# The parts of a group's row maxima in one 128-column tile: one transpose and four small DMAs in place of four transposes and one DMA

## The reference

```
scores  = einsum('bhqd,bhkd->bhqk', q, k) / sqrt(16)      # 4 x 16 x 512 x 512
weights = softmax(scores, axis=-1)
attn    = einsum('bhqk,bhkd->bhqd', weights, v)
```

## Time and profile before

| | us |
|---|---|
| median of 3 runs | 1273.53 (1271.52 to 1274.54) |
| the profiled execution: its own time | 1274.43 |
| its span, first to last instruction | 1272.7 |
| attend stage of xa0, sa0, xa1 (about) | 72 to 340, 414 to 630, 945 to 1155 |
| PE busy | 1131.4 (89% of the span) |
| DVE, ACT, POOL busy | 838.6 (66%), 660.4 (52%), 210.9 (17%) |
| mean granted clock of PE | 0.949 |

### The profile page before, as it was taken

How to read it: one execution, slowest core, us unless ns; L and a number is a source line. 1 busy time by engine, 2 the same in 40 slices (tenths; PEclk the granted TensorE clock), 3 DMA queues, 4 the chain that set the end, 5 groups by cost and what they waited for, 6 DMA issues and landing times. The chain is left out here.

```text
span 1272.7 us, 17810 instructions
## 1 busy us (share of the span) xinstructions
PE 1131.4 (89%) x5693; PEld 544.0 (43%) x5722; DVE 838.6 (66%) x2112; ACT 660.4 (52%) x1341; POOL 210.9 (17%) x272
## 2 busy tenths in 40 slices
PE   7889999999997999999967999996989999998390
PEld 4423343434453223343364666664523333335370
DVE  5878777777478888888762222223888888876722
ACT  3346666666533677677722333332537767674250
POOL 4310000000143000000202222211520010102154
PEclk9989999999999899999967999998989999999795
DMA  8953321221048433543291140103873323211064
GB/s 265 309 169 93 79 57 28 81 52 26 2 154 291 103 91 90 132 97 93 72 375 33 31 161 28 27 13 102 263 241 91 90 59 89 60 37 57 25 171 144
DMA packets 100706, 139.40 MB, mean 110 GB/s; under 512 B 8452, under 2 KB 82632, under 8 KB 99208
## 3 DMA queue, kind: packets, MB, share of 16 engines
q1 hardware_dynamic: 96536, 128.03, 33.6%
q0 software_dynamic: 4080, 10.23, 2.9%
HBM read 86.30 MB, written 52.17 MB: 109 GB/s over the span
## 5 line engine op out<-in xcount | busy, mean ns | idle before, releaser
L885 ACT ACTIVATE r<-ps 128x512 f32<-128x512 f32 x768 | 427.4, 600 | 211.9 <-PE ps L971 122.1
L377 DVE TENSOR_REDUCE m<-ps 128x1 f32<-128x512 f32 x512 | 320.9, 682 | 45.2 <-PE ps L958 44.9
L971 PE MATMUL ps<-r 99*128 99x512 bf16 x768 | 294.3, 388 | 5.6 <-ACT r L885 5.6
L958 PE MATMUL ps<-r 96*128 96x512 bf16 x720 | 280.9, 393 | 20.5 <-DVE m L377 7.0
L373 DVE CUSTOM_DVE_ANT_0 r<-ps,r 128x512 bf16<-128x512 f32 x256 | 170.2, 690 | 60.2 <-PE ps L958 59.6
L985 PE MATMUL ps<-r 128*32 128x512 f32 x1536 | 204.9, 605 | 4.9 <-ACT r L885 3.3
L971 PEld LDWEIGHTS ps<-r 99*128 99x128 bf16 x768 | 74.4, 98 | 211.7 <-ACT r L885 157.3
L958 PEld LDWEIGHTS ps<-r 96*128 96x128 bf16 x720 | 71.3, 99 | 105.9 <-DVE m L377 24.3
L861 POOL COPY r<-r 128x256 f32<-128x256 f32 x48 | 19.0, 399 | 542.1 <-PE ps L985 542.1
L1660 DVE COPY r<-ps 128x512 f32<-128x512 f32 x46 | 31.8, 691 | 91.9 <-PE ps L1707 91.9
L1707 PE MATMUL ps<-r 128*128 x184 | 87.8, 621 | 2.7 <-issue 0.4
(11 more groups left out here) (151 smaller groups left out, 1220.5 us busy)
## 6 DMA issues: line engine op xcount, KB each, us to landing
r<-q_parts SPq DMA_DIRECT2D x48, 384.0 KB, 5.2
r<-k_parts SPq DMA_DIRECT2D x48, 384.0 KB, 6.0
k_parts<-r SPq DMA_DIRECT2D x24, 384.0 KB, 3.3
q_parts<-r SPq DMA_DIRECT2D x24, 384.0 KB, 3.1
r<-in_w SPq DMA_DIRECT2D x16, 512.0 KB, 4.9
r<-in_w SPq DMA_DIRECT2D x8, 1024.0 KB, 14.4
k_parts<-r SPq DMA_DIRECT2D x24, 256.0 KB, 3.3
q_parts<-r SPq DMA_DIRECT2D x24, 256.0 KB, 3.1
```

What stands on the lines that cost most here:

```text
L377: ins = dve.tensor_reduce(out, mem.ps[:, bank, :], AX.X, ALU.max)
L885: act.activation(mem.probs[:, u // HG, u % HG, :], ps[:, ST + (UNITS * g + u) % DEEP, :], ACT.Exp, scale=SCALE).then_inc(a.p_exp.sem, 1)
L958: pe.matmul(ps[:, led_bank(n), :], mem.qst[g][0:ROWS, h, t * P:(t + 1) * P], mem.kst[g][0:ROWS, h, :], start=True, stop=True).then_inc(a.s ...
L971: ins = pe.matmul(out, mem.kst[g][0:KROWS, h, kt * P:(kt + 1) * P], mem.qst[g][0:KROWS, h, :], start=True, stop=not a.masked)
```

## The change

`mparts` becomes a tile of 128 columns, of which 48 carry the parts (4 tiles x 3 parts x 4 heads) and the rest is zero from the start. PE turns it with one transpose: 48 partitions x 128. ACT copies 48 x 128 elements in place of 12 x 512. SP sends the four tiles' parts with four DMAs, each of 12 partitions x 128 (3 KB, in runs of 256 bytes), and the semaphore of the shift counts to 64 in place of 16. POOL has one memset more at the start, and those who wait for the constants wait for 14.

```diff
-        self.mparts = sb("mparts", [P, T, PARTS, HG], BF16)
-        self.mT = sb("mT", [PARTS * HG, S], BF16)
+        self.mparts = sb("mparts", [P, P], BF16)
+        self.mT = sb("mT", [PARTS * T * HG, P], BF16)
...
-        self.shift = [sig(f"shift{s}", 16) for s in range(NG)]
+        self.shift = [sig(f"shift{s}", 16 * T) for s in range(NG)]
...
         sp.wait_ge(a.m_sb.sem, a.m_sb.at(G, 1))
-        sp.dma_start(mem.qst[g][ROWS:KROWS, :, :], mem.mT[:, :]).then_inc(a.shift[g].sem, 16)
+        for t in range(T):
+            sp.dma_start(mem.qst[g][ROWS:KROWS, :, t * P:(t + 1) * P],
+                         mem.mT[t * PARTS * HG:(t + 1) * PARTS * HG, :]).then_inc(a.shift[g].sem, 16)
...
-        act.activation(mem.mT[:, :], ps[0:PARTS * HG, MISC, 0:S // 2].bitcast(BF16), ACT.Copy)\
+        act.activation(mem.mT[:, :], ps[0:PARTS * T * HG, MISC, 0:P // 2].bitcast(BF16), ACT.Copy)\
            .then_inc(a.m_sb.sem, 1)
...
-        for t in range(T):
-            ins = pe.transpose(ps[0:PARTS * HG, MISC, t * P // 2:(t + 1) * P // 2].bitcast(BF16),
-                               mem.mparts[:, t, :, :].rearrange("p a h -> p (a h)"), mem.identb[:, :])
-        ins.then_inc(a.m_ps.sem, 1)
+        pe.transpose(ps[:, MISC, 0:P // 2].bitcast(BF16), mem.mparts[:, :], mem.identb[:, :]).then_inc(a.m_ps.sem, 1)
...
+        mparts = mem.mparts[:, 0:T * PARTS * HG].rearrange("p (t a h) -> p t a h", t=T, a=PARTS)
+        hi, mid, lo = (mparts[:, :, i, :] for i in range(PARTS))
...
+            pool.memset(mem.mparts[:, :], 0.0).then_inc(setup, 1)
```

More of the change, by code:

```diff
@@ L715, in rest_of_batches @@
         if a.fresh:
-            sp.wait_ge(a.setup, 13)
+            sp.wait_ge(a.setup, 14)
             for s in range(NG):
@@ L896, in maxima @@
             b, g = used
-            act.wait_ge(a.shift[g].sem, a.shift[g].at(b, 16))
-        act.activation(mem.mT[:, :], ps[0:PARTS * HG, MISC, 0:S // 2].bitcast(BF16), ACT.Copy)\
+            act.wait_ge(a.shift[g].sem, a.shift[g].at(b, 16 * T))
+        act.activation(mem.mT[:, :], ps[0:PARTS * T * HG, MISC, 0:P // 2].bitcast(BF16), ACT.Copy)\
            .then_inc(a.m_sb.sem, 1)
@@ L966, in transposed_scores @@
         if u == 0:
-            pe.wait_ge(a.shift[g].sem, a.shift[g].at(b, 16))
+            pe.wait_ge(a.shift[g].sem, a.shift[g].at(b, 16 * T))
             if a.masked and g == 0:
@@ L1123, in split @@
         m = mem.m[:, :, :]
-        hi, mid, lo = (mem.mparts[:, :, i, :] for i in range(PARTS))
+        mparts = mem.mparts[:, 0:T * PARTS * HG].rearrange("p (t a h) -> p t a h", t=T, a=PARTS)
+        hi, mid, lo = (mparts[:, :, i, :] for i in range(PARTS))
         dve.tensor_scalar(hi, m, -1.0, None, ALU.mult).then_inc(a.cut.sem, 1)
@@ L1881, in constants @@
             pool.iota(mem.number_i[:, :], [[1, 1]], base=0, channel_multiplier=1).then_inc(setup, 1)
-            pool.wait_ge(setup, 8)
+            pool.wait_ge(setup, 9)
             for eye in (mem.ident, mem.identb):
@@ L2016, in _ @@
             def _(pe):
-                pe.wait_ge(setup, 13)
+                pe.wait_ge(setup, 14)
                 begin, rest = project_tensor(pe, xa0)
```

## The result

The changed kernel takes 1311.8 us (median of 4 runs, 1309.0 to 1313.5), the kernel before on the same chip 1274.0: ratio 1.0298, 95% interval 1.0275 to 1.0321. Forecast were 1306 and 32 us more; it became 38. The profiled execution spans 1310.1 us against 1272.7. The 1311.8 us lie at the upper edge of the forecast's own range of 1296 to 1312.

The account below looks back on a forecast made before the run. PE's order sets the pace, and it waits for operand loads issued behind the shift DMA: sa0 +23.8, xa1 +7.1, xa0 +1.7, together +32.6 us, so 1306 us; own range 1296 to 1312, whole range 1281 to 1330.

Parts of the forecast that it names:

- The mechanism: Attend stages: transposes, copy, shift DMA issue, load and PE form one chain; loads issued 2.02 us later make PE wait.
- the sum: Per group, load delay less slack where positive, else 0.165 us saved: sa0 +23.8, xa1 +7.1, xa0 +1.7, together +32.6 us.
- SP: SP's queue, each group: four shift issues for one at 0.77 us each, 2.31 us more; low bound 1.1.
- rival A: SP's four DMAs issue at the pace of big loads, delay 0.8 us: +8 us, 1282; chance 0.12.
- ACT: ACT's copy of 128 columns in place of 512: about 285 ns, 0.29 us earlier for SP; lower bound 0.195.
- PE: PE, each group: three transposes fewer save 0.165 us, 7.9 us over 48 groups; the 128-column weight load costs nothing.
- The shift rows: Last shift DMA's bytes land at 494.8, PE needs them at 495.79: in time, with 1.0 us left.
- rival D: Shift rows come late; xa1's nine groups with slack lose some 2 us each: +18 on top, 1324; chance 0.05.
- The loads: sa0's 13 loading groups: `k_parts` lands 6.0 to 7.3 us after issue, seven wait already; +24.3 us.
- from 12 us to about 45: Sign of being right: PE's waits for `k_parts` rise so, nearly all in sa0 and xa1's first groups.
- Rival C: PE's clock falls to 0.50 for 11 us in new waits, five falls of about 5.4 us: 27, 1333; chance 0.10.
- Rival B: The loads are hidden, so only PE's 7.9 us saving shows: 1266; chance 0.07.

Follow-up runs that it names:

- DMA part alone: The kernel before, with its four transposes and its copy, but four shift DMAs of 12 x 128 in place of one: 1324.1 us, ratio 1.0403.
- loads-first kernels: Operand loads issued ahead of the shift DMAs: in the changed kernel 1258.4 us, ratio 0.9899; in the kernel before 1268.9 us, ratio 0.9974.
- filler run: The changed kernel plus eight unread matmuls ahead of PE's wait for the operand loads, in 16 groups of sa0 and xa1: 1302.7 us, ratio 1.0225.

## Why the prediction was right, point by point

*The mechanism* was the one forecast: the chain of copy, issues, load and PE. It is shown from three sides: the DMAs alone bring it, the order on SP takes it away with all four DMAs in place, and the number of DMAs doses it. The total came out as near as it did with some luck, since two errors cancelled: PE's saving was mis-sized and the clock falls were left out. By parts, the time lost at the matmuls that wait for `k_parts` (start to start, less 0.22 us) rose by 3.8 us in xa0, 24.6 in sa0 and 11.2 in xa1, where the sum had 3.7, 24.3 and 7.6. The falls add some 10 us to that, and what is left to the stages' +38.4 is a saving of about 11 (up to 1.7 of it from the clock at xa0's start), where the sum had 3.0 in the groups that do not wait.

*SP.* 0.77 us an issue were taken; 0.699 and a gap of 0.04 were measured, 3 x 0.74 = 2.22 us in place of 2.31. The bound from the big loads (rival A) was the wrong neighbour: an issue takes 0.48 us for 384 KB, 0.72 for the old 12 KB and 0.70 for the new 3 KB, so it does not follow the bytes.

*ACT.* 285 ns for the copy by the line through 256 and 512 columns; 264 measured. The first issue came 0.29 us sooner after the transpose in the median of the groups (0.77 in place of 1.06), and 0.21 sooner in the group shown (1.11 in place of 1.32). That the loads came 2.02 us later holds there to the hundredth (5.04 - 3.03 = 2.01), but as the sum of two small misses: SP's block got 2.21 us longer, not 2.31, and its start came 0.21 sooner, not 0.29.

*PE* was mis-sized: 0.165 us a group in the forecast, 0.35 measured. The step that failed is "the one transpose loads 128 columns in place of 12; the wait ahead of it leaves room, and I cost it at nothing": the width is a gain of 0.19. The 0.31 us ahead of the first transpose were to be read in the trace of before as a weight load that was not hidden; I took them for the wait. This is the main reason why xa0, where few groups wait, got 3.1 us shorter and not 1.7 longer (its start also ran less long at 0.50: the granted clock of 66 to 86 us was 0.83 after and 0.74 before, worth up to 1.7 us). In the groups that wait for the load PE's saving is swallowed, as forecast; in the others it did reach the total, and there it hid a good part of what the clock took.

*The shift rows.* They came in time, as forecast from the moved bytes in the earlier trace rows. In the changed kernel the sign of rival D, a wait for `mT`, is there once, with 0.6 us; with the DMA part alone it is 2.6 us in four waits, and in the loads-first kernels it stands at the stages' starts. The Trainium skill's 512-byte rule ("DMA: Bandwidth & Descriptors", Specifications) shows no price here: the kernel with one DMA of 256-byte runs does not wait for it, and in a group without other traffic its bytes move 1.4 to 1.7 us after the issue, as the old runs of 1024 bytes do.

*The loads.* sa0's waits came out as summed. In sa0 the `k_parts` loads landed 4.7 to 7.5 us after their issue, those with a weight load in front not sooner than 6.1; the median of both loads was 6.1, 6.4 before. Some landed later when issued later: the one issued at 1016.8 us in xa1 took 7.5 where it had taken 6.4, which made the longest wait, 4.19 us from one matmul to the next. The sign "from 12 us to about 45" was wrong as it was put: 12 is the sum of PE's two lines with 5 us of lost time in them, and the sum of both lines became 93.7.

*The clock.* Rival C was given 0.10 as a case of its own; in fact it came on top of the forecast, with less than its price: eight falls at some 1.2 us each by the filler run, not five at 5.4, since the clock came back after a few us and not after 11 as at the start of a stage. Among the signs of being wrong was "a granted clock of 0.50 inside a stage", and it came: the forecast had this term at nothing. It is as large as what sa0 and xa1 together took over their forecast (5.9 + 4.6 = 10.5 us). The rule of the Trainium skill ("TensorE: Matmul & The Clock Gate", HAM oscillation), that a DMA wait in each tile brings the clock down again and again, was right here in part: 8 falls beside 22 waits of the matmuls. Forecast and rivals should not have been alternatives: the waits of the one are the cause of the other.

Rival B (1266, loads hidden) did not happen, but kernels that make it true could be written: 1258.4 us with all four DMAs, 1251.6 with one.

## What to carry to other kernels

Ahead of a DMA queue ask what stands behind each issue and who waits for it: here three more issues of 0.74 us a group cost 51 us by themselves, on an engine that computes nothing, and in the changed kernel turning the order round gives back more than it had lost. Prefer one DMA over a few small ones, by choosing the order of the columns ahead of a transpose so that its partitions come out in the order of the destination. Where PE's waits grow (the falls here stood behind waits of 1.6 to 3.8 us, though not behind all of them), price the fall of its clock too, on top of the wait; do not add up the waits of PE's two lines; and look whether a weight load starts beside the matmul ahead of it or after it.

## What the runs showed of the hardware that was not expected

A weight load of 128 columns was hidden behind the running matmul; one of 12 or of 48 columns was not, and neither was the one after it: 0.44 against 0.63 us over four transposes, 0.28 against 0.48 over one. Columns that carry nothing for the result but fill up the tile gain 0.19 to 0.20 us each time in these rows, and 0.11 to 0.16 a group in the length of the stages. Whether a width between 48 and 128 is enough was not tried; loads of 99 x 128 and 96 x 128 were hidden as well as those of 128 x 128, so it is not the number of rows.

Matmuls whose result nobody reads, put into a wait, made a kernel 9 us faster; the clock stayed at 1.00 in the groups that had them.
